# A graph network layer on one core: the next tile's edge products moved from layer 1 into layer 2, and VectorE's low part of their sums moved behind the second residual group

## The reference

```python
h = jnp.maximum(_layernorm(x, axis=-1), 0.0)
agg = segment_sum(edge_features, tgt, N_NODES)
counts = segment_sum(ones, tgt, N_NODES)
agg = agg / jnp.maximum(counts, 1.0)[:, None]
combined = jnp.concatenate([agg, h], axis=1)      # 64 + 256
out = relu(combined @ W1 + b1) @ W2 + b2          # hidden 512, out 256
return x + out
```

## Time and profile before

| | us |
|---|---|
| median of 3 runs | 1332.47 (1331.58 to 1332.96) |
| the profiled execution, its own time | 1333.35 |
| its span, first to last instruction | 1331.8 |
| TensorE matmuls busy | 1323.5 (99%) |
| VectorE busy | 1214.6 (91%) |
| ScalarE busy | 697.0 (52%) |
| GpSimd busy | 542.6 (41%) |
| granted TensorE clock, mean | 0.999 |

### The profile page before, as it was taken

How to read it: one execution, slowest core, us unless ns; L and a number is a source line. 1 busy time by engine, 2 the same in 40 slices (tenths; PEclk the granted TensorE clock), 3 DMA queues, 4 the chain that set the end, 5 groups by cost and what they waited for, 6 DMA issues and landing times.

```text
span 1331.8 us, 29294 instructions
## 1 busy us (share of the span) xinstructions
PE 1323.5 (99%) x7001; PEld 1121.1 (84%) x7001; DVE 1214.6 (91%) x3149; ACT 697.0 (52%) x1285; POOL 542.6 (41%) x710
## 2 busy tenths in 40 slices
PE   8999999999999999999999999999999999999999
PEld 5888888888888888888888888888888888888887
DVE  6999999999999999999999999999999999999997
ACT  5545454545454545454545454545455555555553
POOL 7443434343434343434343434343434343434341
PEclk9999999999999999999999999999999999999999
DMA  4676767675767676767676767676767676767663
GB/s 136 116 142 114 143 112 143 112 141 114 140 115 141 116 140 117 137 119 135 121 135 122 134 122 132 124 130 127 127 129 125 132 123 134 121 136 120 136 111 77
DMA packets 420693, 168.21 MB, mean 126 GB/s; under 512 B 319092, under 2 KB 420230, under 8 KB 420680
## 3 DMA queue, kind: packets, MB, share of 16 engines
q1 hardware_dynamic: 420152, 167.55, 67.5%
q10 hardware_dynamic: 528, 0.52, 0.1%
HBM read 66.25 MB, written 51.40 MB: 88 GB/s over the span
## 4 chain that ended last, share of the span: by engine, by line
PE 98%; DMA 1%; POOL 0%; DVE 0%; SPq 0%; issue 0%; ACT 0%; DVEq 0%; POOLq 0%
PE P L971 27%; PE P L973 14%; PE P L943 14%; PE P L945 13%; PE P L944 13%; PE P L952 7%; PE P L953 7%; PE PA L932 1%; PE PA L931 1%; PE PA L927 0%; DMA dst_w<-in_dst_dram 0%; POOL below L505 0%; DMA table_dram<-table 0%; PE P L1030 0%; DMA DT<-table_dram 0%; DVE H_lo L751 0%
## 5 line engine op out<-in xcount | busy, mean ns | idle before, releaser
L971 PE MATMUL P<-w_both,H_hi 128*128 128x512 f32 x1560 | 546.5, 392 | 0.2
L629 ACT ACTIVATE H_hi<-P 128x512 fp32r<-128x512 f32 x392 | 233.6, 597 | 488.9 <-PE P L953 488.7
L973 PE MATMUL P<-w_both,H_lo 128*128 128x256 f32 x1564 | 438.4, 280 | 0.0
L971 PEld LDWEIGHTS P<-w_both,H_hi 128*128 128x128 f32 x1560 | 292.3, 187 | 65.6 <-DVE H_lo L751 0.9
L751 DVE SCALAR_TENSOR_TENSOR H_lo<-P,H_hi 128x512 fp32r<-128x512 f32 x392 | 265.9, 679 | 70.0 <-ACT H_hi L629 66.6
L943 PE MATMUL P<-HT_hi,w_hi 128*128 128x512 f32 x776 | 309.2, 398 | 0.0
L944 PE MATMUL P<-HT_lo,w_hi 128*128 128x512 f32 x776 | 303.5, 391 | 0.0
L945 PE MATMUL P<-HT_hi,w_lo 128*128 128x512 f32 x776 | 303.4, 391 | 0.0
L479 POOL TENSOR_TENSOR XB<-X,b_row 128x1024 f32<-128x1024 f32 x96 | 231.5, 2412 | 166.5 <-DVE O L766 165.9
L973 PEld LDWEIGHTS P<-w_both,H_lo 128*128 128x128 f32 x1564 | 295.8, 189 | 3.6
L473 POOL TENSOR_TENSOR E_both<-ES,E_both 128x256 fp32r<-128x256 f32 x98 | 72.5, 740 | 389.6 <-ACT E_both L609 389.6
(11 more groups left out here) (95 smaller groups left out, 1208.7 us busy)
## 6 DMA issues: line engine op xcount, KB each, us to landing
out_dram<-O SPq DMA_DIRECT2D x97, 512.0 KB, 4.6
HQ<-HN SPq DMA_DIRECT2D x384, 128.0 KB, 3.9
X<-in_x_dram SPq DMA_DIRECT2D x94, 512.0 KB, 4.2
ER<-in_edge_attr_dram SPq DMA_DIRECT2D x392, 32.0 KB, 1.8
DT<-table_dram SPq DMA_DIRECT2D x392, 1.0 KB, 1.7
X<-in_x_dram ACTq DMA_DIRECT2D x1, 512.0 KB, 5.2
w_raw<-in_L_gnn_W_dram SPq DMA_DIRECT2D x4, 128.0 KB, 3.2
w_raw<-in_L_gnn_W_dram SPq DMA_DIRECT2D x2, 256.0 KB, 4.5
```

The source lines that it names most:

```text
L629: act.activation(H1_hi[:, m, nodes(t)], bank(m)[:, nodes(t)], ACT.Relu).then_inc(s_1hi, 1)
L971: pe.matmul(out_bank(j)[some, :], H1_hi[:, m, rows], w2_both[:, m, :, :].rearrange("p a d -> p (a d)"), start=(m == 0), stop=False)
L973: last = pe.matmul(out_bank(j)[some, 0:D], H1_lo[:, m, rows], w2_both[:, m, 0, :], start=False, stop=(m == CH - 1))
```

## The change

TensorE no longer runs the edge products of the next tile between parts 1 and 2 of layer 1 but in layer 2, behind the fourth pair of group 1, ahead of group 2. So it is now in all tiles that have a next one. VectorE runs `means_low` behind the residual of group 1 instead of group 0. Nothing is added or left out.

```diff
@@ VectorE, step
-                residual(t, b, 0)
-                if later:
-                    means_low(t + 1)
-                for j in groups(t)[1:]:
+                for j in groups(t):
                     residual(t, b, j)
+                    if j == 1 and later:
+                        means_low(t + 1)
@@ TensorE
-            def layer2(t):
+            def layer2(t, b, later):
...
-                    if (j, ms) == (1, (3,)) and isinstance(t, int) and t < 2:
-                        edge_means(t + 1, 1 - t)
+                    if (j, ms) == (1, (3,)) and later:
+                        edge_means(t + 1, 1 - b)
 
             def step(t, b, later=True):
                 for m in range(CH):
                     if not (isinstance(t, int) and t == 0):
                         layer1_nodes(t, b, m)
                     layer1_means(t, m)
-                    if m == 1 and later and not (isinstance(t, int) and t < 2):
-                        edge_means(t + 1, 1 - b)
...
-                layer2(t)
+                layer2(t, b, later)
```

## The result

| | before, us | with the change, us |
|---|---|---|
| median of the runs | 1332.3 (4 runs, 1331.6 to 1333.0) | 1351.9 (4 runs, 1350.6 to 1353.1) |
| profiled execution, its own time | 1333.35 | 1351.37 |
| its span | 1331.8 | 1349.8 |

The ratio is 1.0145, with a 95% interval of 1.0133 to 1.0158: slower by 19.6 us. The forecast was 1350.4, range 1344 to 1357. One of the nine executions of the first experiment, the block alone, ran at a granted clock of 0.557 and took 2197 us, and its ratio leaves that one out.

A forecast was written before the change was run, and what follows sets the result against it. TensorE's stream was taken to set the pace, 13.36 us per tile; the new ring of 13.55 adds 0.19 in 94 tiles, +17.9 us on the median 1332.47, giving 1350.4 us, range 1344 to 1357.

The forecast's parts named there:

- the sum's own bounds: Total loss over 94 tiles, forecast at +17.9 us, with 16.0 to 19.7 us as its lower and upper ends.
- the ring: Per-tile wait chain: third part's last matmul, third H_lo, low part's end, L953, 16 matmuls; 13.55 us against TensorE's 13.36.
- Point 1: TensorE: the seven edge products cost 0.47 us at the old and the new place, so this move alone is worth 0.
- Point 2: VectorE: the means' low part moves behind one more residual group, 0.80 us, and so ends at 612.97.
- Point 4: Layer 1's weight load L952 is 0.29 us late for the low part; TensorE loses 0.17 per tile, +0.19 as a ring.
- Point 5: ScalarE takes up the block's sums 0.28 us later; LayerNorm and transpose DMAs follow, cost 0 with 0.4 us of cover.
- Point 6: Count: the wait arises 94 times, in tiles 2 to 95, none in tile 96; 94 x 0.19 = +17.9 us.
- only the matmul is held, not its load: Rival at layer 1's late weight load: 0.07 us per tile, +6.6, 1339 us; chance 4%.
- Nothing is absorbed: Rival at the late load: its full 0.29 us counts 94 times, +27.3, 1359.7 us; chance 4%.
- No change: Rival: VectorE's tail starts 0.47 us earlier against TensorE and the wait vanishes, 1332.5 us; chance 4%.
- Faster: Rival: the 0.05 us delay at the large matmul behind the block vanishes, 94 x 0.05 = 4.7, 1327.8 us; chance 2%.
- the rival of a swinging clock: Small TensorE holes bring the slower 1.2 GHz level, 1.7 us per tile, +160, 1492 us; chance 1%.

The follow-up runs named there:

- the first experiment: Only the seven edge products moved into layer 2, VectorE's order as in the kernel before: median 1336.3 us, ratio 1.0028 to the kernel before.

## Why the prediction was right

The direction, the mechanism and the size came out as forecast. The 19.6 us lie at the upper end of the sum's own bounds (16.0 to 19.7), and two small errors in the ring, 0.03 us too little in VectorE's leg and 0.02 too much in the 16 matmuls, partly cancelled.

- *Point 1, the block costs 0.47 at either place.* It does by its own rows, 601.51 to 602.21 with the change as before. But the point went on to put the whole move at 0, and that was mis-sized: alone it costs 4.0 us, as the other pairs of layer 2 run 0.003 us slower. Within the change this is hidden, since the ring is longer than TensorE's own 13.40. A forecast for the block alone would have missed it.
- *Point 2, one residual group is 0.80.* The leg from the third H_lo to the low part's end is 8.44, not 8.41. The 0.03 us come with the second transpose of a tile, which takes 1.09 to 1.10 us against 1.06 to 1.08 before, and ScalarE's and VectorE's parts behind it start that much later. The sum gave this leg no bounds. With the low part alone moved it is 8.41, so the 0.03 come with the block's new place; why is open.
- *Point 4, the hand-over and the ring.* 0.41 us to the next L952 instead of 0.40, 3.66 for the 16 matmuls instead of 3.68, 0.31 us of wait by the load's record (forecast 0.3 to 0.35). The ring was forecast at 13.55 and is 13.57; the 94 tiles turn the 0.02 into the 1.8 us between 17.9 and 19.7.
- *Point 5, ScalarE and the moves.* ScalarE's copy of the sums comes later and now waits for TensorE in half of the tiles (11.8 us in all), which costs nothing, because the low part has no wait on it in the loop. The cover of the transposes' DMAs held in all tiles of the loop but two, where VectorE waited 0.3 us for them and the load was 0.6 late (before, one such wait of 0.4); "no wait" was forecast.
- *Point 6, 94 tiles, and no wait from the step of tile 96.* 94 waits; in that step the low part ends at 1338.19, and the load stands at 1338.36.
- *VectorE's idle time* was forecast at 0.8 us before the second and third H_lo: it is 0.33 + 0.48 = 0.81 in one tile and 0.17 + 0.48 = 0.65 in the other.

Of the rivals, "only the matmul is held, not its load" falls by the load's own wait. "Nothing is absorbed" falls by three kernels: loads 0.31, 0.79 and 1.08 us late by their record gave periods of 13.57, 14.00 and 14.33, each 0.14 to 0.15 us less than TensorE's own time at that place (13.40, 13.36, 13.40) and the lateness make together. A late load gave 0.34 to 0.35 us to the next matmul but one each time (610.32 - 609.98, 620.11 - 619.76), against twice 0.23 = 0.46 in an undisturbed stream, so some 0.11 us are absorbed behind the load's start at every size. "No change" falls by the 94 waits. "Faster" falls too: the 0.05 us behind the block did not vanish, they went along, and the first pair behind it takes 0.40 us instead of 0.35. The rule of the Trainium skill (TensorE: Matmul & The Clock Gate, Architectural detail: the array is 16× 32×32), by which loads run ahead of matmuls, fits that part: an undisturbed load starts 0.22 us ahead of its matmul, the late one with it. The clock stayed at 1.00 in six stretches of 200 us from 100 to 1300, with a wait in every tile; one of them, columns as in the earlier trace rows:

```profile
100.00:300.00 200.00, 200.00 (x1044) 166.08 (x1042) 183.40 (x473) 105.68 (x193) 78.63 (x100) 1.00 0.67 125
```

It stayed at 1.00 from 100 to 1300 even with the low part two groups later, where TensorE's matmuls are idle for 0.65 us in every tile. So the rival of a swinging clock has no case here. The section of the Trainium skill behind it (TensorE: Matmul & The Clock Gate, A second HAM failure mode: psum-queue depth-cycling) tells of another kernel, and holes of this size did nothing of the kind here.

## What to carry to other kernels

Where an engine is 99% busy, a reordering is judged by the room of its tightest hand-over, not by its share: follow the ring of waits once round and compare it with the engine's own time per tile. Here the ring had 0.14 us to spare and the hand-over 0.04; one residual group (0.80) was put in and one block (0.47) taken out, which leaves 0.19 over. And follow every ring: a second one, only 0.12 us shorter, kept the place behind part 3 from taking the block out. And a piece of work that is moved has to be checked on both sides: who waits behind it, and whether its own operands are ready at the earlier place.

## What the runs showed of the hardware

- Seven small matmuls cost 0.47 us wherever their operands were ready. The 512- and 256-column pairs of layer 2 took 0.347 us before and 0.350 with the block among them, but also 0.353 in a kernel with the block behind part 3 and a late low part.
- VectorE's masks (128x128, float32 in, from SBUF to SBUF) took 0.28 us each alone and 0.58 to 0.68 us beside GpSimd's two-operand subtraction, which itself went from 0.74 to 0.84 us beside four masks and kept its 0.74 beside one.
- TensorE's wait of 0.3 us per tile (by the load's record) didn't lower its busy share of 99%: matmul records of L951 grew to 0.50 us instead.
- With one mask behind the low part the load was held in every tile read, but for so short a time that the list of waits had 3 of them; only the time from the low part's end to the load, 0.05 to 0.06 us, told the others.
- An undisturbed matmul of 512 columns followed the last by 0.23 us (3.66 for 16). The Trainium skill (TensorE: Matmul & The Clock Gate, Back-to-back issue gap) gives 131 ns for a sustained stream of that width; the measurement decides for these operands.
